# Masking three of fourteen score bundles with matmuls instead of a minimum, and moving six side steps, in a many-head cross attention

## The reference

```python
def _L2_xattn_ref(query, key, value, mask, W_q, W_k, W_v, W_o):
    Q = _split(query @ W_q.T)        # 16 heads of 8 features
    K = _split(key @ W_k.T)          # key = value = context, (32, 1601, 128)
    V = _split(value @ W_v.T)
    scores = jnp.einsum('bhqd,bhkd->bhqk', Q, K) / jnp.sqrt(jnp.float32(D_K))
    scores = jnp.where(mask, -jnp.inf, scores)     # mask (1, 1, 64, 1601), the same for all
    attn_w = jax.nn.softmax(scores, axis=-1)
    attn_w = jnp.nan_to_num(attn_w, nan=0.0)
    out = jnp.einsum('bhqk,bhkd->bhqd', attn_w, V)
    return merged(out) @ W_o.T
```

## Time and profile before

| | |
|---|---|
| median of 3 runs | 3207.23 us (3205.94 to 3211.18) |
| the profiled execution, its own time | 3205.94 us |
| its span in the trace | 3204.1 us |
| mean granted TensorE clock | 0.901 of 2.4 GHz |
| PE busy | 2660.8 us (83%) |
| DVE busy | 2127.0 us (66%) |
| ACT busy | 1388.9 us (43%) |
| POOL busy | 426.1 us (13%) |

### The profile page before, as it was taken

How to read it: one execution, slowest core, us unless ns; L and a number is a source line. 1 busy time by engine, 2 the same in 40 slices (tenths; PEclk the granted TensorE clock), 3 DMA queues, 4 the chain that set the end, 5 groups by cost and what they waited for, 6 DMA issues and landing times. The chain is left out here.

```text
span 3204.1 us, 65263 instructions
## 1 busy us (share of the span) xinstructions
PE 2660.8 (83%) x26294; PEld 1721.6 (54%) x26294; DVE 2127.0 (66%) x6987; ACT 1388.9 (43%) x2527; POOL 426.1 (13%) x299
## 2 busy tenths in 40 slices
PE   7989463796999699999999999999947989888433
PEld 5766352454666456555555555565524555655323
DVE  5554303576111269999999999999756876536776
ACT  3441211464333235555555555554437964334411
POOL 0000102341000000000000000000004960554100
PEclk9999776897999879999999999999768999899766
DMA  7960041000000100000000000000002210991000
GB/s 231 335 204 1 26 131 29 8 3 16 14 14 14 38 21 22 30 25 22 22 22 22 33 22 23 22 22 12 2 8 69 99 60 1 322 352 37 8 0 13
DMA packets 78237, 188.94 MB, mean 59 GB/s; under 512 B 12418, under 2 KB 46149, under 8 KB 77904
## 3 DMA queue, kind: packets, MB, share of 16 engines
q1 hardware_dynamic: 76912, 182.91, 17.3%
q0 software_dynamic: 1024, 1.85, 0.2%
HBM read 154.19 MB, written 30.79 MB: 58 GB/s over the span
## 5 line engine op out<-in xcount | busy, mean ns | idle before, releaser
L3031 DVE CUSTOM_DVE_ANT_0 L_xattn_junk<-L_xattn_ps_mx,L_xattn_shift 128x512 f32<-128x512 f32 (+1 forms) x1024 | 544.6, 569 | 84.2 <-issue 82.1
L3112 ACT ACTIVATE L_xattn_pT<-L_xattn_ps_st 128x512 f32<-128x512 f32 x768 | 416.9, 594 | 406.5 <-PE L_xattn_ps_st L2882 406.4
L2895 PE MATMUL L_xattn_ps_mx<-L_xattn_kT,L_xattn_qb 32*128 32x512 f32 (+1 forms) x2048 | 589.4, 567 | 3.5 <-DVE L_xattn_tops L3031 2.4
L3077 DVE TENSOR_TENSOR L_xattn_pT<-L_xattn_pT,L_xattn_capT 128x512 f32<-128x512 f32 (+1 forms) x896 | 542.3, 646 | 20.8 <-ACT L_xattn_pT L3112 18.7
L2882 PE MATMUL L_xattn_ps_st<-L_xattn_qb,L_xattn_kT 32*128 32x256 f32 (+1 forms) x3328 | 467.5, 394 | 0.0
L2882 PEld LDWEIGHTS L_xattn_ps_st<-L_xattn_qb,L_xattn_kT 32*128 32x128 f32 (+1 forms) x3328 | 295.7, 184 | 19.9
L2942 PE MATMUL L_xattn_ps_pv<-L_xattn_pT,L_xattn_v 128*17 128x128 f32 x6656 | 268.4, 280 | 0.0
L2895 PEld LDWEIGHTS L_xattn_ps_mx<-L_xattn_kT,L_xattn_qb 32*128 32x128 f32 x2048 | 219.0, 188 | 49.9 <-DVE L_xattn_tops L3031 37.7
L2942 PEld LDWEIGHTS L_xattn_ps_pv<-L_xattn_pT,L_xattn_v 128*17 128x17 f32 x6656 | 148.8, 98 | 167.6 <-issue 101.6
L1882 DVE SCALAR_TENSOR_TENSOR x<-L_ffn_ps_o,L_ffn_weights,x 128x128 f32<-128x128 f32 x128 | 36.1, 344 | 224.4 <-PE L_ffn_ps_o L1795 224.4
L2908 PE MATMUL L_xattn_ps_st<-L_xattn_less,L_xattn_ones_b 3*128 3x512 bf16 x768 | 180.0, 390 | 1.4 <-ACT L_xattn_pT L3112 1.2
(11 more groups left out here) (609 smaller groups left out, 4913.5 us busy)
## 6 DMA issues: line engine op xcount, KB each, us to landing
L_xattn_ctxT<-context_turned SPq DMA_DIRECT2D x64, 800.5 KB, 5.6
L_xattn_ctx<-in_ctx SPq DMA_DIRECT2D x64, 768.0 KB
context_turned<-L_xattn_ctxT SPq DMA_DIRECT2D x32, 800.5 KB, 9.7
L_attn_cc<-scratch_rows SPq DMA_DIRECT2D x32, 512.0 KB, 3.7
L_ffn_w<-in_L_ffn_w SPq DMA_DIRECT2D x32, 256.0 KB, 3.1
L_xattn_out_keys<-scratch_q SPq DMA_DIRECT2D x32, 200.1 KB, 10.1
L_ffn_w<-in_L_ffn_W SPq DMA_DIRECT2D x16, 256.0 KB, 3.1
L_xattn_mask<-in_mask_pairs SPq DMA_DIRECT2D x32, 100.1 KB, 14.8
```

What stands on the lines that cost most here:

```text
L2895: last = nc.tensor.matmul(mx[:, w % 3, to:to + width], qb[n % 3][32 * g:32 * g + 32, 2 * (p % 2):2 * (p % 2) + 2, :].rearrange("p h q -> p ...
L3031: last = nc.vector.tensor_tensor_reduce(out=junk[:, w % 3, to:to + width], in0=mx[:, w % 3, to:to + width], in1=shift[:, k0:k0 + width], s ...
L3077: nc.vector.tensor_tensor(x, x, capT[0:k, j[0]:j[1], :].unsqueeze(2).broadcast_to([k, j[1] - j[0], 4, S]), ALU.min)\
L3112: nc.scalar.activation(pT[b % HELD][:, :, gi, :], st[:, w % 3, :].rearrange("p (c k) -> p c k", c=2), ACT.Exp)\
```

## The change

Bundles 2, 6 and 9 of each round are masked by TensorE: `less_out` adds the bf16 mask `shift` to their scores before the exponential, with four matmuls of 64 rows and 256 columns per bundle, and VectorE's minimum for them is left out. V2 and K3 each move one bundle later (2 to 3, and 3 to 4). E1, E2 and E3 move from bundles 4, 6 and 8 to 7, 8 and 9. The side steps then lie at: V1 at 0, K2 at 1, V2 at 3, K3 at 4, V3 at 5, E1 at 7, E2 at 8, E3 at 9, K0 at 10, M at 11, V0 at 12, K1 at 13; none at 2 and 6.

```diff
-    PREPARED = {0: ("K", 0), 2: ("V", 0), 3: ("K", 1), 4: ("V", 1), 5: ("K", 2), 6: ("V", 2), 7: ("K", 3), 9: ("V", 3)}
-    ON_TENSOR = ()
+    PREPARED = {0: ("K", 0), 2: ("V", 0), 3: ("K", 1), 4: ("V", 1), 5: ("K", 2), 7: ("V", 2), 8: ("K", 3), 9: ("V", 3)}
+    ON_TENSOR = (2, 6, 9)
...
-            for kind, at in (("M", -3), ("E1", 18), ("E2", 20), ("E3", 22)):
+            for kind, at in (("M", -3), ("E1", 21), ("E2", 22), ("E3", 23)):
```

## The result

The changed kernel is slower. Its median is 3256.85 us (3253.93 to 3260.91, 4 runs), against 3206.59 us (3205.66 to 3211.18, 4 runs) for the kernel before, a ratio of 1.0154 with an interval of 1.0137 to 1.0172. The profiled execution took 3256.58 us (its span is 3254.8), 50.6 more than the profiled one of before. The forecast was 3184, with a range of 3162 to 3210.

A forecast was written before the change was run, and what follows sets the result against it. TensorE and VectorE bound the kernel jointly, through coupling; after the change TensorE sets the pace nearly everywhere. From 3205.9 us, less 24.6 for 30.7 rounds, plus 3 at the end, gives 3184; range 3162 to 3210.

The forecast's parts named there:

- the walk: Stepping one round bundle by bundle through both engines' work and waits: 36.45 us before, 35.65 after the change.
- The budget of two engines: Work per round before the change: TensorE 32.5 us, VectorE 34.9; the rest of the 36.50 round is coupling.
- the rules (a) to (d): Coupling: (a) maximum 1.17 after bundle start; (b) TensorE 0.63 after VectorE's previous; (c) exponential 1.94; (d) side step awaits `own_values`.
- x: Time four mask matmuls add to TensorE in each of bundles 2, 6 and 9: 0.57 us.
- VectorE alone decides: Rival: TensorE's work overlaps more than its starts show, so the round falls by up to 3.66 us: 3094 us.
- the lower end: Mask matmul time per bundle placed nearer 0.36 us than 1.08, since same-row matmuls follow each other with loads running ahead.
- the slower rival: Both tile shape changes around the mask matmuls cost a full drain, up to 1.08 us per bundle: 3233 us; chance 0.10.
- the 30.7 rounds: Rounds with both engines loaded, where the gain of 0.80 us each holds: 24.6 us in all.
- no change: Rival: mask matmuls add 0.73 to 0.87 us per bundle, round within 0.2 of 36.45, about 3205 us; chance 0.15.
- (d) moves too: E2 at bundle 8 now waits 0.84 us for `own_values`, as long as V3's 0.88 before.
- The clock rival: Clock falls to 1.2 GHz in bundles 2 to 4 every round once bundle 2 lacks its side step: 3286 us; chance 0.03.
- about 3 us lost: Last 18 bundles, without maxima: three masked ones find VectorE idle, so mask matmuls only add time, partly at half clock.

The follow-up runs named there:

- experiment 2: Kernel before, with bundles 2, 6 and 9 masked by TensorE and all side steps left in place: 3193.29 us, 0.9965 of the kernel before.
- 5: Changed kernel with E1 at bundle 6 instead of 7, masks kept: 3173.54 us, 0.9912 of the kernel before.
- 7: Changed kernel with TensorE masks only at 6 and 9, V2 and K3 back in place, E1 and E2 at 6 and 7: 3145.31 us, 0.9828.
- 11: Kernel before, with bundle 2 alone masked by TensorE: 3216.89 us, 1.0046 of the kernel before.
- experiment 3: Changed kernel with eight mask matmuls on 32-row tiles instead of four on 64 (half the queries masked twice, others not): 3167.89 us, ratio 0.9892.
- experiment 8: Kernel before, with only E1, E2 and E3 moved to bundles 7, 8 and 9: 3240.00 us, 1.0107 of the kernel before.
- experiment 4: Changed kernel with six zero-weight matmuls put ahead of E2's wait in bundle 8: 3201.93 us, 0.9978 of the kernel before.
- 9: Changed kernel with all masks on VectorE and six zero-weight matmuls ahead of E2's wait: 3205.47 us, 1.0007 of the kernel before.
- 6: Changed kernel with all masks on VectorE and E1 at bundle 6 instead of 7: 3285.33 us, 1.0254 of the kernel before.
- experiment 1: Changed kernel's six side step moves alone, all masks on VectorE as before: 3241.85 us, 1.0114 of the kernel before.
- experiment 10: Changed kernel with masks on VectorE, E1 at bundle 6 and six zero-weight matmuls ending bundle 7: 3222.88 us, 1.0056 of the kernel before.

## Why the prediction was wrong, step by step

**What bounds the kernel, and the walk: right, to some 0.2 us.** The budget of two engines and the rules (a) to (d), with x as measured, give the round as long as the clock is 1.00. For 2, 5, 7 and 11 the walked figure, or its rounded value, stood in the expectation before the kernel ran; for 3 it is the prediction's own sum for x = 0.43. Measured is the mean from E1 to E1 in the steady part, or the distance that nearly all rounds have:

| kernel | walked | measured |
|---|---|---|
| before | 36.45 | 36.67 |
| 2, masks alone | 36.28 | 36.22 |
| 3, 32 rows | 35.23 | 35.15 |
| 5, E1 at 6 | 35.35 | 35.42 |
| 7, two masks | 34.74 | 34.67 |
| 11, mask at 2 | 37.05 | 37.26 |

The prediction set its walk against a short round. Before, rounds of 36.50 and 36.84 take turns (E1 at 1501.98, 1538.48 and 1575.32), and the walk has nothing of that.

**What is removed: nearly right.** VectorE is busy 31.87 us in a round, where 31.2 was said; so 3.04 left it and not 3.66. The forecast doesn't hang on the rest, since TensorE sets the pace. The rival in which VectorE alone decides is out: experiment 2 takes the same minima away and gains 10 us.

**What is added: the kind right, the size wrong.** "x = 0.57" is 0.75. The step that failed is the reason given for the lower end, that the matmuls' loads can run ahead. They do, but only among the four; 0.31 of the 0.75 goes with the change from 32-row to 64-row tiles and back, and is gone with tiles of 32 rows (experiment 3). What the prediction kept for the slower rival, changes of tile shape, was therefore a term of the sum. By the prediction's own sum, x = 0.75 gives 35.23 + 3 · 0.32 = 36.19, a gain of 0.26 where 0.80 was forecast, some 8 us in the 30.7 rounds. (It called x from 0.73 to 0.87 "within 0.2" of no change; by the same sum 0.73 is 0.32 away.) The rounds without a fall measured 36.29, which is 0.38 under the mean round before. So this alone would have brought the time to the edge of "no change", and not above it.

**What is moved: this is the step that failed.** "(d) moves too ... as long as V3's 0.88 before" is right in size: E2 waits 0.78. But it was priced as 0.84 of TensorE's time wherever it stands. Before, V3 waits 0.88 in bundle 5, whose maxima have 128 keys, and the clock stays at 1.00. Now the wait stands in bundle 8, where the maxima have 65 keys, and in 19 rounds of 27 the clock is at 1.2 GHz for 3.4 or 6.8 us soon after it. That costs 1.79 us a round on the mean (38.08 less 36.29). That it is E1, E2 and E3 that bring it is shown by experiment 8. That closing the gap takes it away is shown by 5, without added work, and by 4 and 9, with it. That E2 need not be the one that waits is shown by 6.

**The clock rival: the right mechanism in the wrong place.** It had 0.03 of the chance and was looked for in bundles 2 to 4, where V2 leaves. Its counter-argument was that bundles 5 to 9 with short steps alone kept 1.00 before. That is so, and there was even a gap of 0.88 among them; but it stood in bundle 5, with 6 and 7 between it and the 65-key ones at 8 and 9, and the change put one into bundle 8. The place which the rival started from, bundles 2 to 4 of the last round, had lost its side steps, and TensorE had no wait listed in the 13 us before its clock fell at 2265. What this should have taught is that the clock can fall in a stream that is listed as busy, and that a share of 1.00 over a stretch says nothing of how near it is to that.

**The sum.** The profiled execution came 73 us over the forecast. The 28 steady distances lack 0.42 each of the forecast gain (0.80 less 0.38), which is 12 us, and take on 1.79 each by the clock, 50 us. The last three distances between E3 and E3 take 101.3 us where they took 89.0 before; with the forecast's small terms for this end that is 11 to 12 more. Together 73, worked out and not measured apart. So the term "about 3 us lost" for the last bundles was too small as well, and no run looked into it. The forecast of no wait at K0, which "waits for that addition, which ends before TensorE gets there", held for the change: no such wait is listed after. It fails in the kernels without masks (experiments 1 and 9).

**What stays open.** What decides whether the clock falls in a given round. The wait of 0.8 at E2 is there in 28 rounds of experiment 3, with the clock falling in four, and in all 27 of the changed kernel, with 19; the rounds of one kernel are alike in their work. Nor does it take a wait of 0.8: experiment 10 falls in seven rounds with 0.36. Filling bundle 8 brought it all back in two kernels and most of it in a third. Which share is due to the wait, to the 65-key bundles, to the work of the filling and to the changes of tile shape was not separated. In "TensorE: Matmul & The Clock Gate", under "A second HAM failure mode", the Trainium skill tells of a kernel in which TensorE's small idle gaps between groups of matmuls made the clock swing between its two levels. The trace agrees in kind, with falls in rounds that have a gap of 0.78 us (the changed kernel) or 1.08 (experiment 1).

## What to carry to other kernels

When a wait moves, price it by where it lands and not by its length alone. Here 0.88 us of idle TensorE in bundle 5 came with no fall of the clock, and 0.78 in bundle 8 cost 1.8 us more a round on the mean. The clock of the stretch before the move gave no warning, since it was 1.00; so read it again after the move, over a few microseconds at a time, and not as a share over the stage. A better place for the step is worth more than a filling (E1 at 6: 83 us back; six matmuls on zero weights in the gap: 55), but the place has to be tried: without the masks the same move of E1 made it worse. Move work from a late engine to another only in stretches where the late engine sets the pace, and count a change of tile shape as a cost of its own: the kernel with two masks placed so gained 1.7%, and the mask at bundle 2 alone lost 0.5%.

## What the runs showed of the hardware

- The granted clock fell to 1.2 GHz in a stretch in which TensorE is listed 98% busy, after a gap of 0.78 us, for 3.4 or 6.8 us at a time, in 19 rounds of 27. The same gap stands in the other eight. Rounds take 36.29 us without a fall, 37.84 with the shorter and 39.39 with the longer.
- Where TensorE has slack later in the round, the fall costs less: 36.68 without, 37.03 and 38.56 with, in experiment 1.
- Six matmuls on zero weights in that gap brought the clock to 1.00: 3256.85 to 3201.93 us, and without masks 3241.85 to 3205.47.
- Going from 32-row tiles to 64-row tiles and back costs 0.31 us here: 0.75 for four matmuls of 64 rows against 0.44 for eight of 32 rows that run in pairs. The weight loads stop for 0.23 and 0.21 us at the two changes.
- Runs of one kernel can lie 20 us apart: 3187.64 to 3206.95 over ten in experiment 4. Its profiled execution took 3205.53 with the clock at 1.00 over the steady part, so falls there don't account for its longer times.
